# GNN and mixture-of-experts kernel: eight of nine additions of finished count tiles as adding transfers from GpSimd's queue

## The chip, the cores and the metric

The kernel runs on one core of one Trainium2 chip. The metric is device time in microseconds (us) of one execution. Differences of 0.5% or so are at the limit of what can be told from no change.

## What is computed

The reference takes x (1250 x 512), and 40000 edges src, dst. Cut to what matters:

```python
h = relu(layernorm(x) @ W1 + b1) @ W2 + b2          # 512 -> 256 -> 512
agg = segment_sum(h[dst], src)                      # row src[e] gets h[dst[e]]
x = x + h + agg
y = layernorm(x)
gate = softmax(y @ Wg + bg) - 0.25 * sigmoid(y @ Wt + bt)
w = max(gate, 0) / sum(max(gate, 0))                # 8 experts
x = x + sum_e w[e] * (y @ We[e] + be[e])
```

## The kernel before, in words

The edges are turned into a matrix of counts: entry (d, s) says how often node s takes from node d, plus one on the diagonal. The aggregation is then a dense product. The matrix has 1250 rows, in ten tiles of 125 (`TILES`), and each tile is made as five blocks (windows, `WPT`) of 25 rows, fifty in all (`NW`). For a block w

- VectorE (`compare`, L632) compares edge keys with positions and writes one-hot matrices into a ring of buffers,
- TensorE (`count`, L892 and L900) multiplies them and collects the counts in a PSUM bank, two banks in turn,
- ScalarE (`block_out`, L426) copies the bank to the buffer `counts[w % 5]`, once that buffer's last contents have been moved, and writes the positions of block w + 5 (L394),
- SP (L316) issues a copy of 125 KB from `counts[q]`, which lies as (position, 250), into 25 rows of the tile `a_t[i % 3]`. Three tiles are buffered; before the first block of tile i >= 3 SP waits until tile i - 3 has been aggregated (`g_done`) and summed.

TensorE takes up the aggregation of tile i (`aggregate`, L862: r_sb, the hidden layer, times the tile, added up in ps_g) ten blocks after the tile's first block, in pieces between the counting of blocks. Tiles 8 and 9 are aggregated after the last block, with no counting between.

The bias b2 enters with a factor, the number of terms a row has: the column sums of the whole count matrix. For this the ten tiles are added up in `a_sum` (125 x 1250, fp32; `column_sum`, L657), and ten small matmuls with a column of ones (L925) give the degrees. VectorE copies them (L678) and adds `b2 * degree` to x tile by tile (L684, ten instructions), before the output of the second layer is added (L692) and the second layer norm and the experts follow. In VectorE's program the additions of tiles 1 to 7 stand among the comparisons, that of tile 8 behind the last comparison, and that of tile 9 behind the low part of the first expert's weights (`low_weights`, L672). TensorE waits for the last addition after two of the six pieces of tile 9.

`a_t` and `a_sum` lie in the tensor `late`, and this is how the profile names them. The expert bias is broadcast to the same place afterwards (L321). GpSimd sets constants at the start and has nothing to do afterwards; it issues no transfer.

Of the kernel before, what the change touches and what calls it, by code (L numbers as in the profile page):

```python
# [16 lines left out]
ALU = mybir.AluOpType  # L17
# [13 lines left out]
def gnn_moe(nc, x, src, dst, W1, b1, W2, b2, Wg, bg, Wt, bt, We, be, out):  # L31
# [4 lines left out]
    TILES = 10  # L36
# [11 lines left out]
    WPT = 5  # L48
# [22 lines left out]
    with ExitStack() as ctx:  # L71
# [3 lines left out]
        def sem(name):  # L75
            return ctx.enter_context(nc.semaphore(name))
# [85 lines left out]
        a_t = [late[:, i * SW:(i + 1) * SW] for i in range(3)]  # L162
        a_sum = late[:, 3 * SW:4 * SW]
# [56 lines left out]
        step_base, step_ready, step_prep = sem("step_base"), sem("step_ready"), sem("step_prep")  # L220
        win_done, win_out = sem("win_done"), sem("win_out")
        win_moved = [sem(f"win_moved{q}") for q in range(WPT)]
        a_summed = sem("a_summed")
        g_done = sem("g_done")
        we_hi_done, we_lo_done = sem("we_hi_done"), sem("we_lo_done")
        wg_hi_done, wg_lo_done = sem("wg_hi_done"), sem("wg_lo_done")
# [43 lines left out]
        def moved(eng, tile):  # L270

            for q in range(WPT):
                eng.wait_ge(win_moved[q], 16 * (tile + 1))
# [11 lines left out]
        @block.sync  # L285
        def _(sp):
            sp.dma_start(dst_i[:, :, :], dst.rearrange("(j g e) -> g j e", j=GJ, e=EP)).then_inc(dst_in, 16)
            sp.dma_start(src_i[:, :, :], src.rearrange("(j g e) -> g j e", j=GJ, e=EP)).then_inc(src_in, 16)
            for j in range(TILES // 2):
                if j == 1:  # L290
                    sp.dma_start(w1_sb[:, :, :], W1.rearrange("(k p) c -> p k c", p=128)).then_inc(w1_in, 16)
                sp.dma_start(x_sb[0:112, 2 * j:2 * j + 2, :],
                             x[2 * j * R:(2 * j + 2) * R, :].rearrange("(t p) d -> p t d", p=R)[0:112, :, :]).then_inc(x_in[j], 16)
            sp.dma_start(b1_all[:, :], b1.partition_broadcast(R)).then_inc(b1_in, 16)

            def load_expert(e):
                sp.dma_start(stage[e % 2][:, :].rearrange("p (k f) -> p k f", k=KD),
                             We[e, :, :].rearrange("(k p) f -> p k f", p=128)).then_inc(we_in[e % 2], 16)

            sp.dma_start(w2_sb[:, :, :], W2.rearrange("(k p) c -> p k c", p=128)).then_inc(w2_in, 16)  # L300
            sp.dma_start(b2_sb[:, :], b2.partition_broadcast(R)).then_inc(b2_in, 16)
            sp.dma_start(wg_sb[:, :, 0:EXP], Wg.rearrange("(k p) c -> p k c", p=128)).then_inc(wg_in, 16)
            sp.dma_start(wg_sb[:, :, EXP:G1], Wt.rearrange("(k p) c -> p k c", p=128),
                         allow_slow_non_contiguous=True).then_inc(wg_in, 16)
            sp.dma_start(bg_sb[:, 0:EXP], bg.partition_broadcast(R)).then_inc(bg_in, 16)
            sp.dma_start(bg_sb[:, EXP:G1], bt.partition_broadcast(R)).then_inc(bg_in, 16)
            load_expert(0)
            load_expert(1)

            for w in range(NW):  # L310
                i, q = w // WPT, w % WPT
                sp.wait_ge(win_out, w + 1)
                if q == 0 and i >= 3:
                    sp.wait_ge(g_done, i - 2)
                    sp.wait_ge(a_summed, max(i - 3, 1))
                sp.dma_start(a_t[i % 3][q * WIN:(q + 1) * WIN, :].rearrange("p (h l) -> p h l", h=HI),  # L316
                             counts[q][0:WIN * HI, :]).then_inc(win_moved[q], 16)

            sp.wait_ge(g_done, TILES)
            sp.wait_ge(deg_done, 1)  # L320
            sp.dma_start(be_sb, be.rearrange("e f -> (e f)").partition_broadcast(R).rearrange("p (e f) -> p e f", e=EXP)).then_inc(be_in, 16)  # L321
            for e in range(2, EXP):
                sp.wait_ge(we_lo_done, e - 1)
                load_expert(e)

            for i in range(TILES):
                sp.wait_ge(acc_step, TILES * (EXP - 1) + i + 1 + RING)
                sp.dma_start(out[i * R:i * R + 112, :], x_sb[0:112, i, :]).then_inc(out_sent, 16)
            sp.wait_ge(out_sent, 32 * TILES)

        @block.gpsimd
        def _(pool):
# [26 lines left out]
            for n in range(len(STEPS) - 1, 0, -1):  # L359
# [4 lines left out]
                if len(STEPS) - len(FIXED) < n:  # L364
# [12 lines left out]
                                    base=-(HI - 1), pattern=[[1, SEG + HI - 1]], channel_multiplier=-HI).then_inc(self_ready, 1)  # L377
            nc.gpsimd.affine_select(out=self_lo[0:WIN, :], in_=self_lo[0:WIN, :], compare_op=ALU.not_equal, fill=1.0,
                                    base=-(LO - WIN), pattern=[[1, 2 * LO - WIN]], channel_multiplier=-1).then_inc(self_ready, 1)

        @block.scalar
        def _(act):
# [136 lines left out]
        def _(dve):  # L519
# [88 lines left out]
            def first_norm(n):  # L608

                if n == 0:  # L610
                    centre()
                if n < TILES // 2:
                    statistics(n)
                if n in RSTD_AT:
                    rstd(RSTD_AT[n])
# [33 lines left out]
                    step_done()  # L649
                dve.reg_mov(end_reg[w % 4], turn_reg)  # L650

            def column_sum(i):

                moved(dve, i)
                if i > 1:
                    dve.wait_ge(a_summed, i - 1)
                nc.vector.tensor_tensor(a_sum, a_t[0] if i == 1 else a_sum, a_t[i % 3], ALU.add).then_inc(a_summed, 1)  # L657

            for w in range(NW):
                compare(w)  # L660
                if w in NORM_AT:
                    first_norm(NORM_AT[w])
                if w >= 3 * WPT + 1 and (w - 1) % WPT == 0:
                    column_sum((w - 1) // WPT - 2)
            column_sum(TILES - 2)

            dve.wait_ge(wg_hi_done, 1)
            nc.vector.scalar_tensor_tensor(out=wg_2[:, :, G1:2 * G1], in0=wg_sb[:, :, :], scalar=WSCALE,
                                           in1=wg_2[:, :, 0:G1], op0=ALU.mult, op1=ALU.subtract).then_inc(wg_lo_done, 1)
            def low_weights(e, par):  # L670
                dve.wait_ge(we_hi_done, e + 1)
                nc.vector.scalar_tensor_tensor(out=we_lo[par][:, :], in0=stage[par][:, :], scalar=WSCALE, in1=we_hi[par][:, :],  # L672
                                               op0=ALU.mult, op1=ALU.subtract).then_inc(we_lo_done, 1)

            low_weights(0, 0)
            column_sum(TILES - 1)
            dve.wait_ge(deg_done, 1)
            nc.vector.tensor_copy(deg1[:, :], ps_a[0:R, 0:TILES]).then_inc(deg_ready, 1)  # L678
            dve.wait_ge(deg_ready, 1)
# [117 lines left out]
        def _(pe):  # L797
# [57 lines left out]
            def aggregate(i, first, last, closes=None):  # L855

                if first == 0:
                    moved(pe, i)
                    pe.wait_ge(r_ready, i + 1 if i > 0 else TILES)
                for n, (c, a, z) in enumerate(cuts[first:last]):  # L860
                    opens = i == 0 and (first + n == 0 or a // BANK != cuts[first + n - 1][1] // BANK)
                    g = nc.tensor.matmul(ps_g[:, a:z], r_sb[:, i, c * 128:(c + 1) * 128], a_t[i % 3][:, a - c * SW:z - c * SW],  # L862
                                         start=opens, stop=False, skip_group_check=True)
                    if n == 0 and closes is not None:
                        g.then_inc(win_done, 1)
                if last == len(cuts):
                    g.then_inc(g_done, 1)
# [52 lines left out]
                    aggregate((w - WPT - LAG) // WPT, piece, piece + 1 if piece < WPT - 1 else len(cuts), closes=w)  # L920
            aggregate(TILES - 2, WPT - LAG, len(cuts))
            aggregate(TILES - 1, 0, 2)
            pe.wait_ge(a_summed, TILES - 1)
            for i in range(TILES):
                dg = nc.tensor.matmul(ps_a[0:R, i:i + 1], a_sum[:, i * R:(i + 1) * R], ones[0:R, 0:1], start=True, stop=True)  # L925
            dg.then_inc(deg_done, 1)
# [108 lines left out]
```

## Time and profile before

| | |
|---|---|
| time, median of 3 runs | 393.59 us (392.02 to 393.86) |
| profiled execution | 392.6 us, its span 390.8 us |
| busy | TensorE 369.8, VectorE 286.8, ScalarE 105.3, GpSimd 6.1 us |
| counting and aggregation | from about 33 to 144 us |
| DMA | 23.87 MB in 16808 packets, mean 61 GB/s |

The span is what the profiler's records cover; the execution's own time is 1.8 us longer. Busy time is that of an engine's own instructions; waits and DMA issues don't count. The DMA share of a stretch is the mean busy share of the core's sixteen DMA engines.

### The profile page before, as it was taken

How to read it: one execution, taken by the hardware profiler on the slowest of the kernel's cores; microseconds unless marked ns; L12 is line 12 of the kernel's file. 1: busy time of each engine (PE TensorE's matmuls, PEld its weight loads, DVE VectorE, ACT ScalarE, POOL GpSimd, SP SyncE). 2: the span in 40 equal slices, each digit the busy share in tenths (PEclk: the TensorE clock that was granted, in tenths of full speed). 3: DMA queues.
4: the chain of work that ended last, by engine and by line, in shares of the span. 5: the costliest groups of instructions: out<-in, count | busy, mean ns of one | idle time of the engine just before them, and what ended most of it. 6: DMA issues, size and time to landing. Idle time of an engine off the chain costs nothing.

```text
span 390.8 us, 5935 instructions
## 1 busy us (share of the span) xinstructions
PE 369.8 (95%) x1892; PEld 240.8 (62%) x1892; DVE 286.8 (73%) x440; ACT 105.3 (27%) x189; POOL 6.1 (2%) x33
## 2 busy tenths in 40 slices
PE   0999999999999999979999999999999999999996
PEld 0777787656556563566566666666666666666663
DVE  3799987999988949872895756756767558566653
ACT  4734355556666204554001010010010100100000
POOL 6000000000000000000000000000000000000000
PEclk9999999999999999987999999999999999999999
DMA  8970011222222206300030020300301200000223
GB/s 175 243 239 17 15 39 37 78 67 80 74 73 83 83 14 160 132 28 2 1 107 2 10 99 0 108 0 0 107 0 23 84 0 0 0 0 0 68 91 105
DMA packets 16808, 23.87 MB, mean 61 GB/s; under 512 B 2796, under 2 KB 9683, under 8 KB 16660
## 3 DMA queue, kind: packets, MB, share of 16 engines
q1 hardware_dynamic: 16382, 23.05, 20.0%
q10 hardware_dynamic: 403, 0.53, 0.6%
q8 instruction: 12, 0.20, 0.2%
q14 instruction: 11, 0.09, 0.1%
HBM read 14.77 MB, written 2.56 MB: 44 GB/s over the span
## 4 chain that ended last, share of the span: by engine, by line
PE 80%; DVE 11%; issue 3%; DVEq 2%; DMA 1%; ACT 1%; ACTq 0%
PE ps_g L974 18%; PE ps_g L975 17%; PE ps_g L976 17%; PE ps_g L862 9%; PE ps_w L900 8%; DVE split L632 3%; PE ps_g L848 2%; PE ps_g L938 2%; DVE x_sb L684 2%; DVE stats L597 2%; DMA dst_i<-in_dst_dram 1%; PE ps_w L892 1%; PE ps_a L948 1%; DVEq L648 1%; PE ps_g L850 1%
## 5 line engine op out<-in xcount | busy, mean ns | idle before, releaser
L974 PE MATMUL ps_g<-we_hi,split 128*125 128x512 f16 x320 | 122.3, 382 | 0.4 <-DVE x_sb L758 0.4
L975 PE MATMUL ps_g<-we_lo,split 128*125 128x512 f16 x320 | 122.0, 381 | 0.0
L976 PE MATMUL ps_g<-we_hi,split 128*125 128x512 f16 x320 | 122.0, 381 | 0.0
L758 DVE SCALAR_TENSOR_TENSOR x_sb<-ps_g,weight_s,x_sb 125x512 f32<-125x512 f32 x80 | 59.9, 749 | 56.2 <-PE ps_g L976 56.1
L632 DVE TENSOR_TENSOR split<-places,keys 125x1536 f16<-125x1536 int16 (+2 forms) x125 | 91.3, 794 | 7.8 <-PE ps_w L900 4.2
L763 DVE SCALAR_TENSOR_TENSOR x_sb<-late,weight,x_sb 125x512 f32<-125x512 f32 x80 | 59.9, 750 | 9.5 <-DVE x_sb L758 5.5
L974 PEld LDWEIGHTS ps_g<-we_hi,split 128*125 128x125 f16 x320 | 44.1, 138 | 26.2 <-DVE x_sb L758 0.8
L976 PEld LDWEIGHTS ps_g<-we_hi,split 128*125 128x125 f16 x320 | 44.0, 137 | 25.8 <-issue 0.6
L975 PEld LDWEIGHTS ps_g<-we_lo,split 128*125 128x125 f16 x320 | 44.0, 138 | 25.4 <-issue 0.6
L900 PE MATMUL ps_w<-split 125*128 125x250 f16 x402 | 53.7, 270 | 3.4 <-DVE split L632 1.8
L900 PEld LDWEIGHTS ps_w<-split 125*128 125x128 f16 x402 | 36.8, 97 | 22.4 <-issue 9.7
L495 ACT ACTIVATE we_hi<-stage 128x2048 f16<-128x2048 f32 x6 | 11.5, 1912 | 139.8 <-PE ps_g L976 139.8
L862 PE MATMUL ps_g<-late,r_sb 125*128 125x512 f32 (+3 forms) x120 | 49.0, 515 | 0.0
L394 ACT ACTIVATE places<-iota_pos,win_base 125x512 int16<-125x512 int16 x50 | 35.7, 715 | 0.0
L426 ACT ACTIVATE counts<-ps_w 128x250 f32<-128x250 f32 x50 | 19.0, 380 | 32.7 <-PE ps_g L862 27.9
L862 PEld LDWEIGHTS ps_g<-late,r_sb 125*128 125x128 f32 x120 | 19.5, 191 | 7.7 <-issue 7.1
L848 PE MATMUL ps_g<-w_sb,x_t 128*125 128x256 f32 x80 | 19.6, 388 | 0.0
L672 DVE SCALAR_TENSOR_TENSOR we_lo<-stage,we_hi 128x2048 f16<-128x2048 f32 x8 | 18.3, 2284 | 0.0
L657 DVE TENSOR_TENSOR late<-late 125x1250 f32<-125x1250 f32 x9 | 13.1, 1456 | 4.4 <-DMA late<-counts 4.3
L848 PEld LDWEIGHTS ps_g<-w_sb,x_t 128*125 128x125 f32 x80 | 14.2, 187 | 1.8
L938 PE MATMUL ps_g<-w_sb,early 128*125 128x512 f32 x32 | 14.8, 595 | 0.1
L892 PE MATMUL ps_w<-self_lo,self_pos 128*128 128x250 f16 x50 | 13.6, 273 | 0.7 <-ACT counts L426 0.7
(129 smaller groups left out, 193.0 us busy)
## 6 DMA issues: line engine op xcount, KB each, us to landing
stage<-in_L_ffn_W_exp_dram SPq DMA_DIRECT2D x8, 1024.0 KB, 5.3
late<-counts SPq DMA_DIRECT2D x50, 122.1 KB
x_sb<-in_x_dram SPq DMA_DIRECT2D x5, 448.0 KB, 11.2
out_dram<-x_sb SPq DMA_DIRECT2D x10, 224.0 KB
late<-in_L_ffn_b_exp_dram SPq DMA_DIRECT2D x1, 2000.0 KB
w_sb<-in_L_gnn_W_dram SPq DMA_DIRECT2D x2, 512.0 KB, 11.6
x_sb<-in_x_dram ACTq DMA_DIRECT2D x1, 260.0 KB
out_dram<-x_sb ACTq DMA_DIRECT2D x10, 26.0 KB
```

The source lines that it names most:

```text
L394: nc.scalar.activation(places[w % WPT][:, :, 0:SEG], iota_pos[:, :, :], ACT.Identity, bias=win_base[:, w:w + 1], scale=1.0).then_inc(pos_r ...
L426: nc.scalar.activation(counts[q][:, :], ps_w[w % 2][:, 0:LO], ACT.Copy).then_inc(win_out, 1)
L632: nc.vector.tensor_tensor(hot[hot_at(w, p)][:, 0:n, :].rearrange("p c (k x j) -> p (c k) x j", k=SEGS, j=2), places[w % WPT][:, 0:n, :].re ...
L758: nc.vector.scalar_tensor_tensor(out=x_sb[:, i, :], in0=ps_exp[(TILES * par + i) % RING], scalar=weight_s[:, ds(e, 1), i], in1=x_sb[:, i, ...
L763: nc.vector.scalar_tensor_tensor(out=x_sb[:, i, :], in0=be_sb[:, ds(e, 1), :], scalar=weight[:, i, ds(e, 1)], in1=x_sb[:, i, :], op0=ALU.m ...
L848: nc.tensor.matmul(r_bank[i % 2], x_t[i % XTS][:, k, :], w1_sb[:, k, :], start=(k == 0), stop=False)
L862: g = nc.tensor.matmul(ps_g[:, a:z], r_sb[:, i, c * 128:(c + 1) * 128], a_t[i % 3][:, a - c * SW:z - c * SW], start=opens, stop=False, ski ...
L900: mm = nc.tensor.matmul(bank[:, 0:LO], hot[hot_at(w, p)][:, c, 0:SEG], hot[hot_at(w, p)][:, c, SEG:SEG + LO], start=False, stop=False, ski ...
L938: y = nc.tensor.matmul(ps_y[i % YS], g_sb[:, c, tokens[i]], w2_sb[:, c, :], start=(c == 0), stop=(c == KC - 1))
L974: nc.tensor.matmul(bank, xhi[:, k, tokens[i]], hi_w, start=(k == 0), stop=False)
L975: nc.tensor.matmul(bank, xhi[:, k, tokens[i]], lo_w, start=False, stop=False)
L976: mm = nc.tensor.matmul(bank, xlo[:, k, tokens[i]], hi_w, start=False, stop=(k == KD - 1))
```

## The change

A semaphore `a_added` is new. GpSimd, after its constants, issues nine transfers of whole tiles (125 x 1250 fp32): tile 0 is copied to `a_sum`, tiles 1 to 8 are added to it by the transfer (`accum_op=ALU.add`). Each waits until its tile's five blocks have landed and until the transfer before it is complete. VectorE keeps the addition of tile 9, at its old place, and waits there for all nine. SP waits for the transfers instead of VectorE's sums before it fills a buffer again. TensorE waits for the one count that VectorE now gives.

```diff
--- before.py
+++ after.py
@@ -220,7 +220,7 @@
         step_base, step_ready, step_prep = sem("step_base"), sem("step_ready"), sem("step_prep")
         win_done, win_out = sem("win_done"), sem("win_out")
         win_moved = [sem(f"win_moved{q}") for q in range(WPT)]
-        a_summed = sem("a_summed")
+        a_added, a_summed = sem("a_added"), sem("a_summed")
         g_done = sem("g_done")
         we_hi_done, we_lo_done = sem("we_hi_done"), sem("we_lo_done")
         wg_hi_done, wg_lo_done = sem("wg_hi_done"), sem("wg_lo_done")
@@ -312,7 +312,7 @@
                 sp.wait_ge(win_out, w + 1)
                 if q == 0 and i >= 3:
                     sp.wait_ge(g_done, i - 2)
-                    sp.wait_ge(a_summed, max(i - 3, 1))
+                    sp.wait_ge(a_added, 16 * (i - 2))
                 sp.dma_start(a_t[i % 3][q * WIN:(q + 1) * WIN, :].rearrange("p (h l) -> p h l", h=HI),
                              counts[q][0:WIN * HI, :]).then_inc(win_moved[q], 16)
 
@@ -377,6 +377,13 @@
                                     base=-(HI - 1), pattern=[[1, SEG + HI - 1]], channel_multiplier=-HI).then_inc(self_ready, 1)
             nc.gpsimd.affine_select(out=self_lo[0:WIN, :], in_=self_lo[0:WIN, :], compare_op=ALU.not_equal, fill=1.0,
                                     base=-(LO - WIN), pattern=[[1, 2 * LO - WIN]], channel_multiplier=-1).then_inc(self_ready, 1)
+
+            for i in range(TILES - 1):
+                moved(pool, i)
+                if i > 0:
+                    pool.wait_ge(a_added, 16 * i)
+                nc.gpsimd.dma_start(a_sum[:, :], a_t[i % 3][:, :],
+                                    accum_op=ALU.bypass if i == 0 else ALU.add).then_inc(a_added, 16)
 
         @block.scalar
         def _(act):
@@ -649,20 +656,10 @@
                     step_done()
                 dve.reg_mov(end_reg[w % 4], turn_reg)
 
-            def column_sum(i):
-
-                moved(dve, i)
-                if i > 1:
-                    dve.wait_ge(a_summed, i - 1)
-                nc.vector.tensor_tensor(a_sum, a_t[0] if i == 1 else a_sum, a_t[i % 3], ALU.add).then_inc(a_summed, 1)
-
             for w in range(NW):
                 compare(w)
                 if w in NORM_AT:
                     first_norm(NORM_AT[w])
-                if w >= 3 * WPT + 1 and (w - 1) % WPT == 0:
-                    column_sum((w - 1) // WPT - 2)
-            column_sum(TILES - 2)
 
             dve.wait_ge(wg_hi_done, 1)
             nc.vector.scalar_tensor_tensor(out=wg_2[:, :, G1:2 * G1], in0=wg_sb[:, :, :], scalar=WSCALE,
@@ -673,7 +670,9 @@
                                                op0=ALU.mult, op1=ALU.subtract).then_inc(we_lo_done, 1)
 
             low_weights(0, 0)
-            column_sum(TILES - 1)
+            moved(dve, TILES - 1)
+            dve.wait_ge(a_added, 16 * (TILES - 1))
+            nc.vector.tensor_tensor(a_sum, a_sum, a_t[(TILES - 1) % 3], ALU.add).then_inc(a_summed, 1)
             dve.wait_ge(deg_done, 1)
             nc.vector.tensor_copy(deg1[:, :], ps_a[0:R, 0:TILES]).then_inc(deg_ready, 1)
             dve.wait_ge(deg_ready, 1)
@@ -920,7 +919,7 @@
                     aggregate((w - WPT - LAG) // WPT, piece, piece + 1 if piece < WPT - 1 else len(cuts), closes=w)
             aggregate(TILES - 2, WPT - LAG, len(cuts))
             aggregate(TILES - 1, 0, 2)
-            pe.wait_ge(a_summed, TILES - 1)
+            pe.wait_ge(a_summed, 1)
             for i in range(TILES):
                 dg = nc.tensor.matmul(ps_a[0:R, i:i + 1], a_sum[:, i * R:(i + 1) * R], ones[0:R, 0:1], start=True, stop=True)
             dg.then_inc(deg_done, 1)
```

## Rows read from the trace of the kernel before

**Rows 1.** The page, parts 1, 2 and 4: engines, slices, chain.
```profile
PE 369.8 (95%) x1892; PEld 240.8 (62%) x1892; DVE 286.8 (73%) x440; ACT 105.3 (27%) x189; POOL 6.1 (2%) x33
...
POOL 6000000000000000000000000000000000000000
...
PE 80%; DVE 11%; issue 3%; DVEq 2%; DMA 1%; ACT 1%; ACTq 0%
```

**Rows 2.** Chain of waits, 103 to 144 us (start, us, what).
```profile
103.19 0.54 PE ps_w L900 x5
...
107.19 0.19 issue
107.38 0.38 ACT counts L426
...
127.44 0.54 PE ps_w L900 x5
...
131.49 0.43 issue
...
133.21 0.26 issue
...
134.17 7.60 PE ps_g L862 x20
141.77 2.09 PE ps_a L925 x20
```

**Rows 3.** The chain, 60 to 84 us.
```profile
78.75 0.93 DVE late L657
...
81.95 0.60 PE ps_w L900 x4
```

**Rows 4.** Timeline, 130 to 156 us (start, length, what, idle before).
```profile
129.55 3.11 DVE L632 TENSOR_TENSOR split<-places,keys 125x768 f16<-125x768 int16 x5
...
134.06 2.28 DVE L672 SCALAR_TENSOR_TENSOR we_lo<-stage,we_hi 128x2048 f16<-128x2048 f32 x1
...
139.79 1.46 DVE L657 TENSOR_TENSOR late<-late 125x1250 f32<-125x1250 f32 x1 [3.45 <-DMA late<-counts]
...
144.09 6.71 DVE L684 SCALAR_TENSOR_TENSOR x_sb<-b_sb,deg,x_sb 125x512 f32<-125x512 f32 x10
...
146.47 0.29 SPq L321 DMA_DIRECT2D late<-in_L_ffn_b_exp_dram  x1
...
146.81 0.39 SPq L297 DMA_DIRECT2D stage<-in_L_ffn_W_exp_dram  x1
```

**Rows 5.** One line's instructions, L657: duration min/median/max in ns.
```profile
L657 DVE TENSOR_TENSOR late<-late x9: 1451/1454/1461, 78.7 to 139.8; 125x1250 f32<-125x1250 f32 x9
```

**Rows 6.** Timeline, 81 to 83.5 us.
```profile
81.09 0.42 PEld L900 LDWEIGHTS ps_w<-split 125*128 125x128 f16 x4 [0.33 <-DVE split L632]
...
81.95 0.33 PEld L900 LDWEIGHTS ps_w<-split 125*128 125x128 f16 x4 [0.43 <-DVE split L632]
81.95 0.60 PE L900 MATMUL ps_w<-split 125*128 125x250 f16 x4 [0.16 <-DVE split L632]
```

**Rows 7.** Timeline of SP's queue, three of the fifty count copies.
```profile
68.46 0.74 SPq L316 DMA_DIRECT2D late<-counts  x1
...
127.07 0.74 SPq L316 DMA_DIRECT2D late<-counts  x1
...
135.54 0.74 SPq L316 DMA_DIRECT2D late<-counts  x1
```

**Rows 8.** Stretches: length, busy (instructions) by engine, granted clock, DMA share, GB/s.
```profile
core 0: us, PE busy (x) PEld busy (x) DVE busy (x) ACT busy (x) POOL busy (x), PEclk, DMA share, GB/s
100.00:130.00 30.00, 28.77 (x157) 17.53 (x156) 27.43 (x42) 19.25 (x38) 0.00 (x0) 1.00 0.27 80
160.00:165.00 5.00, 5.00 (x33) 2.96 (x32) 4.21 (x13) 2.94 (x6) 0.00 (x0) 1.00 0.31 134
160.00:180.00 20.00, 17.85 (x107) 11.75 (x106) 12.97 (x37) 10.23 (x20) 0.00 (x0) 0.83 0.13 53
```

## The prediction

> **What bounds the kernel now.** I read the page first: TensorE is busy for 95% of the span, VectorE for 73%, GpSimd for 2%, and the chain of work that ended last is 80% TensorE and 11% VectorE [rows 1]. The change touches only the stretch from about 58 to 150 us, so I asked for the chain of waits there. Between 103 and 134 us it is TensorE's counting and aggregation matmuls, broken by "issue" and ScalarE pieces of 0.1 to 0.4 us, and no VectorE piece [rows 2]. VectorE stands in it only before 82 us, where the first addition has 0.93 us [rows 3]. Behind the last block the order turns around: ten accumulations end at 141.77, the degree matmuls (L925) run to 143.86, VectorE copies the degree, and its ten L684 instructions fill 144.09 to 150.80 (6.71 us) [rows 2, 4]. That is the tail: whoever delays the full sum delays everything behind it, one for one. So two questions decide: does anything in 58 to 134 us wait for an addition now, and is the sum ready as early as before?
>
> The profiled execution took 392.6 us, 1.8 more than its span of 390.8, and 1.0 less than the median of 393.59. I add the change to 392.6 and carry the difference over to the median.
>
> **What is removed.** Eight of nine VectorE additions at 1.454 us, 11.6 us in all [rows 5]. In rows 2 none of them is on the chain. At 82 us there is one real stall: TensorE idles 0.16 us for VectorE's comparisons at 81.95, and weight loads before it are held 0.33 and 0.43 us [rows 6]; the first addition, 3 us earlier, pushed those comparisons back. I book a gain of 0.2 us, and at most 0.93. Later VectorE is ahead: its comparisons of the last block ended at 129.55 + 3.11 = 132.66, and TensorE took them up at 133.47 [rows 4]. Behind the last comparison the eighth addition lies before the weights' low part L672, which ends at 136.34, and VectorE then idles 3.45 us for the last transfer [rows 4]: nothing to gain. What is late next, in each of these places, is TensorE itself.
>
> **What is added.** One copy and eight adding transfers of 125 rows of 5000 bytes, 625 KB each, on GpSimd's queue. GpSimd has nothing behind them: it does 6.1 us of work in all [rows 1]. But three others wait for them:
> - each addition waits for the one before (same destination), so they form a row of nine;
> - SP waits for addition i-3 before it issues the first count copy of tile i. Behind that instruction stand all later count copies, for which ScalarE (reuse of the count buffer) and TensorE (accumulation) wait;
> - VectorE waits for the ninth before its own last addition, and TensorE's degree matmuls wait for that; behind them are the last four accumulations of tile 9.
>
> The trace has no adding DMA, so I bound its length A. Fixed part: the last count copy is issued at 135.54 and VectorE can go on at 139.79, 4.25 us later [rows 4, 7]. One such copy is 125 KB on five engines (below), 25 KB each, which at 18.5 GB/s is 1.35 us; so 2.9 us are fixed. Moving part: an addition has to read two tiles and write one, 1.25 MB of reads. Rates: from 160 to 165 us what is left of the loads issued at 146.5 and 146.8 [rows 4] is the broadcast of the expert bias, with a DMA share of 0.31, that is 5.0 of 16 engines, and 134 GB/s: 26.8 GB/s per busy engine. From 100 to 130 us the count copies have a share of 0.27 (4.3 engines) at 80 GB/s: 18.5 GB/s per busy engine [rows 8]. On sixteen engines the moving part is 1.25 MB / 16 = 78 KB per engine, 2.9 us at the first rate and 4.2 at the second; if the second operand were free, 1.5 us. On five it is 250 KB, 9.3 to 13.5 us. So A is between 2.9 + 1.5 = 4.4 and 2.9 + 13.5 = 16.4. I take sixteen engines, the split that favours the change, and A = 6.5; five is a rival. In time alone this is hidden: tile 1 is complete at 68.46 + 4.25 = 72.7 us, the last sum begins at 139.8, eight additions in a row fit as long as A is under (139.8 - 72.7) / 8 = 8.4 us; tile 8 is complete at 127.07 + 4.25 = 131.3, and with 6.5 its addition ends at 137.8.
>
> One rule speaks to the choice. The bias rows are 125 to a transfer, and it ran on 5.0 engines [rows 8]. The Trainium skill, "DMA: Bandwidth & Descriptors", section "Why a DMA increments its semaphore by 16 and not by 1", says the number of engines is the largest divisor up to 16 of the outer dimension; by that rule, the trace agrees (125 gives 5). The same section says that GpSimd's queue gives some direct copies all sixteen with the rows rounded up per engine; no row here shows it. The first would make the addition the rival of five engines (about 424 us), the second leaves the forecast.
>
> **The engines are the scarce part.** The count copies are on five engines, which are therefore 86% busy (4.3 of 5) in the stretch [rows 8]. The time per tile is three tiles from 103.19 to 127.44, 8.1 us each [rows 2]. On each of the five engines a tile's copies take 125 KB, 6.8 us at 18.5 GB/s; part of that is waiting inside a packet, since at 26.8 GB/s it would be 4.7. An addition on sixteen engines lays 2.9 to 4.2 us on the same five. The sum is 7.6 at best, below 8.1: nothing is late; 11.0 at worst, 2.9 too much. I take the middles, 5.8 + 3.55 = 9.35: 1.25 us too much per tile. Seven tiles (2 to 8) pass while an addition runs, so the last tile lands 8.75 us late. First the copies' time to landing eats this up, then ScalarE's wait for a free count buffer holds TensorE back, but both ways the last landing is late by all of it, because there is no room in the tail: accumulations of tile 9 begin at 141.77 - 1.72 (four pieces of 0.43) = 140.05, and its last copy lands at 139.79: 0.3 us [rows 2, 4]. The final sum ends at 141.25 against 141.77, 0.5 us.
>
> Sum: + 8.75 - 0.3 (room) - 0.2 (VectorE's stall) = + 8.2, rounded to 8. 392.6 + 8 = 400.6 for an execution like the profiled one, 393.59 + 8 = 401.6 against the median. Own range of this case: + 3 (1.25 replaced by 0.5) to + 20 (2.9 per tile), so 396.6 to 413.6. TensorE would idle for some microseconds in such a stall; the mean granted clock, 1.00 in the rows before, is 0.83 from 160 to 180 us [rows 8], where TensorE is busy for 17.85 of 20 us. A second such stretch, at the same lost share (0.17 of 20 us), would add 3.4 us; it is in the range, not in the sum.
>
> A second rule bears on the read of both tiles. The Trainium skill, "Collectives: The Full Stack", section "The bandwidth ceiling: the fold count and why AG ≠ RS ≠ AR", says that a DMA engine's addition costs a second source read and not the arithmetic. No row here shows it. By it the 2.9 stands; if the second read were free the load would be 5.8 + 1.5 = 7.3, under 8.1, and the next rival would be the forecast.
>
> **Rivals.**
> - *Hidden.* The additions fit into the gaps of the five engines (7.6 us or less per tile). For it: a share of 0.27 with 18.5 GB/s means that the packets wait for each other, and another queue could use that time. Against: 86% busy. In the tail the ninth addition shares the engines with the last three copies, 2.9 us at most, of which I let 1 us reach the landing: + 1.0 - 0.2 = + 0.8, 394.4 us.
> - *Row of nine too long.* The adding transfer runs on five engines as the bias load does. A = 2.9 + 9.3 = 12.2, over the 8.4 from which it decides; the ninth ends at 72.7 + 8 x 12.2 = 170.3, 30.5 late. SP's wait holds the copies back meanwhile, but the row is the longer. 393.6 + 30.5 = 424 us; at the slower rate (A = 16.4) 64 late, 457.6.
> - *Faster.* VectorE was behind TensorE's small stalls after all. The chain's pieces that are not matmul between 107.15 and 133.47 are ten, of 0.02 to 0.43 us (the longer ones stand in [rows 2]), 1.9 us together, and with the 0.2 it is 2.1: 391.5 us. It decides if no comparison is ready when TensorE asks. Against: a comparison is 0.8 us ahead in the last block, and the pieces stand behind the shortest accumulations, where TensorE waits for ScalarE to free a bank. This is the other side.
> - *Not what it says:* GpSimd could reach its first transfer late, so that nothing overlaps. Its own work is 6.1 us, all of it in the first of 40 slices [rows 1], so I give this nothing.
>
> **How the numbers follow.** Forecast 0.40, of which 0.04 comes out within 0.5%; hidden 0.28, 0.25 of it within 0.5% and 0.03 above; five engines 0.24; faster 0.08, of which 0.06 by over 0.5% and 0.02 under. An effect of 0.5%, 2.0 us, is about what a measurement of this kernel can tell from none. Hence faster 0.06; within 0.31; slower 0.63. The range goes from 392.8, which leaves out about 0.09 below (the faster case and the edge of the hidden one), to 426, which leaves out the part of the five-engine case with the slower rate, about 0.11.
>
> **What would show it.** The DMA queue of GpSimd in the queue table, nine issues, and the DMA share of 100 to 130 us: 0.45 or more if sixteen engines work, under 0.35 if five. Copies' landings: the idle of VectorE before its last sum, 3.45 us before, longer by the loss, put down to the landing of a count copy (forecast) or to the adding transfer (row too long). Time per tile in the chain: 8.1 if hidden, above 9 in the last tiles if the engines are full. VectorE's busy time should fall by 11.6 us and the 0.16 us at 82 should go. The forecast is wrong if the share stays far below 0.45 while the tiles keep their 8.1 us, and the start of the degree matmuls, 141.77, is within 1 us of that.

## The result, and the profile after

The changed kernel takes 425.92 us (median of four, 422.17 to 427.94) against 392.80 before (four executions); the ratio is 1.084, 95% interval 1.0785 to 1.0896: 33 us slower. The profiled execution took 427.94 us, its span 426.1 us against 390.8. Ratios leave out an execution that was slow against others of its kernel: of e5's ten one (992.65 us), and e4, with one of its two slow, has no ratio.

The page of the changed kernel, parts 1 to 4 (busy time; the span in 40 slices; DMA queues; the chain):

```profile
PE 381.7 (90%) x1892; PEld 245.2 (58%) x1892; DVE 277.5 (65%) x432; ACT 105.2 (25%) x189; POOL 13.5 (3%) x42
...
DMA  8860132675676665063000202020020300000133
...
q1 hardware_dynamic: 16382, 23.05, 18.4%
q0 software_dynamic: 1296, 5.63, 11.4%
...
PE 67%; DMA 21%; DVE 6%; issue 3%; DVEq 1%; ACT 1%; ACTq 0%; POOLq 0%
PE ps_g L973 16%; PE ps_g L975 16%; PE ps_g L974 16%; DMA late<-counts 14%; DMA late<-late 5%; PE ps_w L899 4%; PE ps_g L937 3%; PE ps_g L861 3%; DVE split L639 2%; PE ps_g L847 2%; DVE stats L604 1%; DMA dst_i<-in_dst_dram 1%; PE ps_w L937 1%; ACT counts L433 1%; PE ps_a L924 1%
```

DMA is now 21% of the chain (1% in [rows 1]), and most of it, 14%, is put down not to the new transfers but to the old count copies (`late<-counts`). VectorE's busy time is 9.3 us less, not 11.6: the additions are gone, but its other instructions, the comparisons among them, take somewhat longer. The chain in the stretch (start, length in us), which answers to [rows 2]:

```profile
73.50 12.52 DMA late<-counts
...
91.63 8.77 DMA late<-counts
...
102.15 11.04 DMA late<-counts
...
120.30 9.41 DMA late<-counts
...
130.13 8.18 DMA late<-counts
...
138.74 11.55 DMA late<-counts
...
150.39 13.44 DMA late<-late
...
164.39 7.77 DMA late<-late
...
172.28 1.47 DVE late L675
...
173.80 3.11 PE ps_a L924 x20
176.91 5.14 PE ps_g L861 x8
```

The count copies on the chain take 8 to 12.5 us. From issue to landing, all copies issued from the first addition on (72.67) take 4.3 to 14.4 us; before, the longest took 4.75. They queue behind each other, up to five at a time. The degree matmuls, at 141.77 before [rows 2], start at 173.80: 32.0 us of the span's 35.3. The other 3.3 lie behind them. There the degree matmuls take 3.11 us instead of 2.09, and the granted clock is down while TensorE waits (stretches as in [rows 8]: length, busy time by engine, clock, DMA share, GB/s):

```profile
100.00:130.00 30.00, 23.84 (x122) 13.97 (x122) 17.57 (x28) 15.80 (x31) 2.51 (x3) 0.94 0.73 118
160.00:176.00 16.00, 6.73 (x24) 3.44 (x22) 1.46 (x1) 0.00 (x0) 0.83 (x1) 0.76 0.42 66
```

The DMA share of 100 to 130 us has risen from 0.27 to 0.73. GpSimd's queue gives the time per tile (start, length of the issue, and the wait before it):

```profile
100.95 0.84 POOL L385 DMA_DIRECT2D late<-late  x1 [11.30 <-DMA late<-counts]
112.33 0.83 POOL L385 DMA_DIRECT2D late<-late  x1 [10.54 <-DMA late<-counts]
...
136.75 0.83 POOL L385 DMA_DIRECT2D late<-late  x1 [12.42 <-DMA late<-counts]
150.39 0.84 POOL L385 DMA_DIRECT2D late<-late  x1 [12.81 <-DMA late<-counts]
164.39 0.83 POOL L385 DMA_DIRECT2D late<-late  x1 [13.16 <-DMA late<-counts]
```

From one issue to the next it is 16.1 and 12.2 us for the first two intervals (from the issue at 72.67), then 11.9 each for three, and 13.6 and 14.0 for the last two, against 8.1 before. An adding transfer takes 11.5 us from issue to landing (the page's median; 10.6 to 13.4, and 7.8 for the last).

The profile says that GpSimd waited for count copies. The landings in the trace (the semaphore's events) say otherwise from tile 4 on: the tile had landed, and the transfer was issued 0.56 us after the one before it had landed.

| tile | its copies landed | transfer before landed | issued |
|---|---|---|---|
| 2 | 88.16 | 85.14 | 88.80 |
| 4 | 108.39 | 111.77 | 112.33 |
| 6 | 132.30 | 136.19 | 136.75 |
| 8 | 154.22 | 163.83 | 164.39 |

So the last 60 us before the final sum are the row of transfers, one after the other, and the count copies are late beside it. At the end (TensorE, then VectorE):

```profile
168.17 3.74 PE L861 MATMUL ps_g<-late,r_sb 125*128 125x512 f32 x4 [7.38 <-DMA late<-counts]
173.80 3.11 PE L924 MATMUL ps_a<-ones,late 125*125 125x1 f32 x20 [1.89 <-DVE late L675]
172.28 1.46 DVE L675 TENSOR_TENSOR late<-late 125x1250 f32<-125x1250 f32 x1 [25.11 <-DMA late<-late]
```

The last count copy lands at 167.93, 28.4 us later than before (139.57). Less the 0.3 us of room, plus 2.0 for the four accumulations at the lower clock (3.74 instead of 1.72 us) and TensorE's wait of 1.89 us for the sum, that makes the 32.0 us.

### The profile page after: what moved, and what is told of

Same layout as the page of the kernel before. It is cut to its first block, busy times and chain, and to the rows that moved or that the text cites. A ratio compares the mean times of both kernels' runs of the same rounds, so it can differ in the third digit from the quotient of the medians.

```text
span 426.1 us, 5933 instructions
## 1 busy us (share of the span) xinstructions
PE 381.7 (90%) x1892; PEld 245.2 (58%) x1892; DVE 277.5 (65%) x432; ACT 105.2 (25%) x189; POOL 13.5 (3%) x42
## 3 DMA queue, kind: packets, MB, share of 16 engines
q1 hardware_dynamic: 16382, 23.05, 18.4%
## 4 chain that ended last, share of the span: by engine, by line
PE 67%; DMA 21%; DVE 6%; issue 3%; DVEq 1%; ACT 1%; ACTq 0%; POOLq 0%
PE ps_g L973 16%; PE ps_g L975 16%; PE ps_g L974 16%; DMA late<-counts 14%; DMA late<-late 5%; PE ps_w L899 4%; PE ps_g L937 3%; PE ps_g L861 3%; DVE split L639 2%; PE ps_g L847 2%; DVE stats L604 1%; DMA dst_i<-in_dst_dram 1%; PE ps_w L937 1%; ACT counts L433 1%; PE ps_a L924 1%
## 5 line engine op out<-in xcount | busy, mean ns | idle before, releaser
L639 DVE TENSOR_TENSOR split<-places,keys 125x1536 f16<-125x1536 int16 (+2 forms) x125 | 92.4, 795 | 29.4 <-PE ps_w L899 11.4
L899 PE MATMUL ps_w<-split 125*128 125x250 f16 x402 | 55.0, 277 | 11.5 <-issue 9.3
L861 PE MATMUL ps_g<-late,r_sb 125*128 125x512 f32 (+3 forms) x120 | 54.7, 566 | 8.4 <-DMA late<-counts 8.4
L502 ACT ACTIVATE we_hi<-stage 128x2048 f16<-128x2048 f32 x6 | 11.5, 1911 | 139.4 <-PE ps_g L975 139.4
L861 PEld LDWEIGHTS ps_g<-late,r_sb 125*128 125x128 f32 x120 | 21.6, 210 | 18.3 <-issue 16.5
L891 PE MATMUL ps_w<-self_lo,self_pos 128*128 128x250 f16 x50 | 14.1, 281 | 6.6 <-ACT counts L433 6.6
L675 DVE TENSOR_TENSOR late<-late 125x1250 f32<-125x1250 f32 x1 | 1.5, 1461 | 25.1 <-DMA late<-late 25.1
## 6 DMA issues: line engine op xcount, KB each, us to landing
late<-late POOLq DMA_DIRECT2D x9, 610.4 KB, 11.5
```

The source lines that it names most:

```text
L639: nc.vector.tensor_tensor(hot[hot_at(w, p)][:, 0:n, :].rearrange("p c (k x j) -> p (c k) x j", k=SEGS, j=2), places[w % WPT][:, 0:n, :].re ...
L899: mm = nc.tensor.matmul(bank[:, 0:LO], hot[hot_at(w, p)][:, c, 0:SEG], hot[hot_at(w, p)][:, c, SEG:SEG + LO], start=False, stop=False, ski ...
```

## The experiments

Theory A: the transfers fill the DMA engines that the count copies need, and the copies land late whether anyone waits for a sum or not. Theory B: the engines have room; the loss is in the waits, nine transfers in a row, SP's wait and VectorE's. The edits are shown shortened: setup, and semaphore counts that follow from the edit, are left out.

**e1, the load without the waits.**

```diff
+ junk_in, junk_sum = sb("junk_in", [R, SW]), sb("junk_sum", [R, SW])
  (kernel before; on GpSimd:)
+ for i in range(TILES - 1):
+     moved(pool, i)
+     if i > 0: pool.wait_ge(a_added, 16 * i)
+     nc.gpsimd.dma_start(junk_sum, junk_in, accum_op=bypass if i == 0 else add).then_inc(a_added, 16)
```

> The kernel before, with VectorE's nine additions and all its waits, plus nine extra transfers of the same size from GpSimd's queue, triggered by the same landings, but between two spare tiles of their own; nothing waits for them. Theory A, full engines: in the changed kernel a row of 5000 bytes that is added holds a DMA engine for 0.65 to 0.75 us (its packets), eight rows are 6.0 us on each of sixteen engines, and with the 5.8 to 6.8 us of a tile's count copies on five of them that is 12 to 13 us per 8.1 us tile; so the load alone must cost most of the 33 us: 410 to 426. Theory B, the waits: each addition takes about 11 us, over the 8.4 that fit in a row of nine, and SP and VectorE wait for them; without waits the time is that of before, 391 to 395.

423.28 us, ratio 1.078 (1.0705 to 1.0862). The load alone, between tiles that nobody reads, costs nearly what the change costs (31.2 us of 33, with overlapping intervals); waits are not needed for the loss, and B is out as the main cause. The chain holds the same long count copies, and no transfer of GpSimd's:

```profile
73.56 12.62 DMA late<-counts
...
93.27 9.11 DMA late<-counts
102.80 9.81 DMA late<-counts
...
126.25 11.75 DMA late<-counts
```

**e2, the waits without the load.**

```diff
- nc.gpsimd.dma_start(a_sum[:, :], a_t[i % 3][:, :], ...)
+ part = SW if i == 0 else 25
+ nc.gpsimd.dma_start(a_sum[:, 0:part], a_t[i % 3][:, 0:part], ...)
```

> The changed kernel with all its waits; the copy of tile 0 stays whole, the eight additions take 25 of 1250 columns (the rest of the sum is left out, so the degrees are wrong). Theory A: with 100 bytes per row the engines are free, 391 to 395. Theory B says the same if the length of an addition is what counts. Theory C, that the waits, the issue from GpSimd's queue and the turn from one transfer to the next cost by themselves (some 4 us each, on SP's path): 397 or more.

392.53 us, ratio 1.000 (0.997 to 1.004). Waiting on GpSimd's queue costs nothing by itself; theory C is out.

**e3 and e4, the dose.** The same edit with `accum_op=ALU.bypass` for all nine, and with `part = SW // 2`.

> The changed kernel with all nine transfers as plain copies (nothing is added, the degrees are wrong): same rows, same waits. The one copy in the changed kernel held an engine 0.35 us per row. Theory A: 8 rows x 0.35 to 0.45 = 2.8 to 3.6 us, with 5.8 to 6.8 of the count copies 9 to 10 per tile against 8.1: 1 to 2 us x 7 tiles, 400 to 407. Theory B: the copy took 5.5 us from issue to landing, under 8.4: 392 to 395.

> The changed kernel, the copy of tile 0 whole, the eight additions over 625 of 1250 columns (half of the sum is left out). Theory A: 8 rows x 0.37 = 3 us per engine, like the plain copies: 399 to 407. Theory B: an addition takes about 6 to 7 us, under the 8.4 that fit: 392 to 395. If the cost is per row and not per byte, 415 or more.

Copies: 406.85 us, ratio 1.037 (1.031 to 1.042). Half the columns: 397.0 and 403.9 us in two runs, too far apart for an interval, both above before. The copies are where A put them (400 to 407) and B did not; of the halves one run is in A's 399 to 407, the other 2 us under it and 2 above B's. A copy and half an addition take nearly the same time on an engine (e6), and in the traces the last count copy is late by nearly the same: 8.3 and 7.0 us.

**e6, the price by itself.** The kernel before, with seven transfers between spare tiles late in the expert phase.

```diff
+ pool.wait_ge(exp_done, 55)
+ copy 125x1250; add 125x1250; copy; add; add 125x625; add 125x25; add 125x1250 with max_dma_last_dim=1000
+ (each after the one before)
```

> The kernel before; in the late expert phase, where no other transfer is under way, GpSimd issues seven transfers between two spare tiles, one after the other: copy, addition, copy, addition of 125 x 1250, addition of 125 x 625, of 125 x 25, and an addition of 125 x 1250 cut into 1000-byte pieces. If an addition is slow by itself: 8 rows x 0.7 us + 3 = 8 to 9 us against 5.5 for the copy, 5 to 6 for the half. If it was slow only because of the count copies beside it: 6 us. The cut one: about 8.5 on sixteen engines, 20 on five. Time of the kernel as before, 390 to 394.

GpSimd's queue (start, issue, wait before):

```profile
322.76 0.75 POOL L391 DMA_DIRECT2D junk_sum<-junk_in  x1 [314.14 <-PE ps_g L989]
328.03 0.90 POOL L391 DMA_DIRECT2D junk_sum<-junk_in  x1 [4.52 <-DMA junk_sum<-junk_in]
336.00 0.55 POOL L391 DMA_DIRECT2D junk_sum<-junk_in  x1 [7.07 <-DMA junk_sum<-junk_in]
...
348.95 0.84 POOL L391 DMA_DIRECT2D junk_sum<-junk_in  x1 [7.07 <-DMA junk_sum<-junk_in]
353.72 0.83 POOL L391 DMA_DIRECT2D junk_sum<-junk_in  x1 [3.93 <-DMA junk_sum<-junk_in]
356.06 3.10 POOL L391 DMA_DIRECT2D junk_sum<-junk_in  x1 [1.50 <-DMA junk_sum<-junk_in]
```

The kernel's time is that of before (one execution, 392.64 us). Start to start: the copy 5.3 us, the addition 8.0, the half 4.8, the 25 columns 2.3. The engines' rate within a transfer (clock, DMA share, GB/s at the end of each row; first an addition, then a copy, then half an addition):

```profile
330.00:335.00 5.00, 5.00 (x25) 3.17 (x24) 3.01 (x4) 0.00 (x0) 0.00 (x0) 1.00 0.91 108
337.50:339.50 2.00, 2.00 (x11) 1.28 (x10) 1.50 (x2) 0.00 (x0) 0.00 (x0) 1.00 1.02 255
...
351.00:353.00 2.00, 2.00 (x11) 1.23 (x9) 1.85 (x3) 0.00 (x0) 0.00 (x0) 1.00 0.89 115
```

With nothing beside it an addition fills 0.91 of sixteen engines at 108 GB/s, 625 KB in 5.8 us; a copy runs at 255 GB/s, 2.45 us; half an addition at 115, 2.7 us. (A share of 1.02 shows that packets can overlap in this count; it is rough.) So the slow addition of the changed kernel is not only slowed by its neighbours: 8.0 of its 11.5 us are its own. The cut one took 19.1 us to land, with transfers of the kernel's own beside it from 365 us on; the share does not say on how many engines.

**e7, smaller rows.**

```diff
+ for h in range(HI):
+     nc.gpsimd.dma_start(a_sum[:, h * LO:(h + 1) * LO], a_t[i % 3][:, h * LO:(h + 1) * LO], ...)
```

> The changed kernel, each tile's transfer issued as five transfers of 125 x 250 (1000 bytes per row) that are under way together. Same bytes, same rule of who waits. If the loss is the bytes' time on the engines (5.6 us of additions + 5.8 of copies per 8.1 us tile): 415 to 428 again. If it is that a count packet of 46 ns stands behind one addition row of 0.6 us each time, the smaller rows let the copies through: 395 to 408.

432.37 us, ratio 1.101 (1.092 to 1.111), above both ranges. The smaller rows do let count copies through while an addition runs. The trace has a record for each packet. Those of 1000 bytes on the copies' queue from 75 to 81 us, during the first addition:

| kernel | count packets in 6 us |
|---|---|
| before | 401 |
| changed (rows of 5000 bytes) | 35 |
| e7 (rows of 1000 bytes) | 190 |

In the changed kernel 105 rows of the addition pass in the same time; a third of them, 33, would be on five of sixteen engines (an estimate), so one count packet goes through for about each row. But no time is gained in e7: from tile 3 on each tile's transfers are issued when those of the tile before have landed, and they take 11 to 15 us (the last ones 7.3). The bytes' time stays, and five issues per tile keep GpSimd busy for 11.23 of the 30 us from 100 on. Rows of 1000 bytes on sixteen engines, without the waits, were not tried.

**e8, fewer engines at a time.** e1 with `max_dma_last_dim=1000`.

> As the load-only kernel (nothing waits for the extra transfers), but each cut into 1000-byte pieces, which I expect to put it on five engines instead of sixteen, not always the five of the count copies. If the loss comes from sharing DMA engines, only those transfers cost that meet the copies' five engines, so a third or less of the 31 us: 394 to 404, with most copies landing in 3.3 to 4.5 us. If it comes from the memory or the fabric in common, 415 or more.

418.76 us, ratio 1.067 (1.059 to 1.074); I expected 394 to 404, and missed. By its time alone the run speaks for the rival, a memory or a path in common (415 or more). What is seen in the trace speaks against it: between 66 and 170 us count copies hold the chain three times, twice while the fourth transfer is under way (issued at 115.09) and once during the fifth (140.26), and never during the second and third. First the chain, then GpSimd's queue:

```profile
117.73 9.36 DMA late<-counts
127.52 10.52 DMA late<-counts
145.47 12.49 DMA late<-counts
```

```profile
75.21 3.03 POOL L389 DMA_DIRECT2D junk_sum<-junk_in  x1 [14.99 <-DMA late<-counts]
93.83 3.02 POOL L389 DMA_DIRECT2D junk_sum<-junk_in  x1 [15.60 <-DMA late<-counts]
115.09 3.02 POOL L389 DMA_DIRECT2D junk_sum<-junk_in  x1 [18.24 <-DMA late<-counts]
140.26 3.03 POOL L389 DMA_DIRECT2D junk_sum<-junk_in  x1 [22.16 <-DMA late<-counts]
```

Two stretches, during the second transfer and during the fourth (clock, DMA share, GB/s of all queues at the end):

```profile
79.00:92.00 13.00, 12.13 (x73) 7.53 (x70) 13.00 (x18) 6.42 (x14) 0.00 (x0) 1.00 0.63 110
119.00:136.00 17.00, 13.52 (x63) 6.86 (x62) 9.59 (x15) 6.27 (x13) 0.00 (x0) 0.91 0.41 71
```

In the first, 62 count packets go through per microsecond (67 before, in the same stretch); in the second 35 (80 before), though less moves in all, 71 against 110 GB/s. A memory in common that was full would hold the copies where most moves. That some transfers hurt and others don't fits engines shared or not; where a transfer does meet the copies, it holds them for some 20 us, which my estimate lacked. The records of the trace don't name the engine, so this stays a reading. The last count copy lands 18.4 us late; the rest of the 26.8 us lies behind it, and what it is wasn't looked into.

**e9, SP's wait relaxed.** `late` one tile larger, `a_t[i % 4]`, SP waits from tile 4 on for addition i - 4.

> The changed kernel with four buffered count tiles instead of three, so that SP waits for the addition of tile i-4 before it fills a buffer. Theory A, full engines: SP's wait is a symptom, the engines stay full, 418 to 427. Theory B, what is left of it: SP's wait (10.1 us in the trace of the changed kernel) and TensorE behind it; then 10 us less, 412 to 418.

424.10 us, ratio 1.080 (1.074 to 1.087): the interval overlaps that of the changed kernel. SP's wait is worth nothing that can be told in the whole time. In the trace it does show: the last count copy lands at 162.58, not 167.93, but VectorE then still waits for the ninth transfer, to 167.21.

**e5, VectorE relieved, nothing put in its place.**

```diff
-                if w >= 3 * WPT + 1 and (w - 1) % WPT == 0:
-                    column_sum((w - 1) // WPT - 2)
-            column_sum(TILES - 2)
  (SP's wait for the sums goes too)
```

> The kernel before without the first eight additions and without any transfer in their place: VectorE adds tiles 8 and 9 once, at the end (the rest of the sum is left out). This is the most that relieving VectorE can bring. My step: 0.2 us, at most 0.93, so a ratio of 0.998 to 1.001. Rival, the small stalls of TensorE between 103 and 134 us were VectorE's: 2 us less, ratio 0.995.

Ratio 1.001 (0.998 to 1.003). Eight additions on VectorE cost nothing, so there was nothing to win by moving them anywhere.

**e10, GpSimd's own adder.**

```diff
- nc.gpsimd.dma_start(a_sum, a_t[i % 3], accum_op=...)
+ nc.gpsimd.tensor_tensor(a_sum, a_t[0] if i == 1 else a_sum, a_t[i % 3], ALU.add)
```

> The kernel before with tiles 1 to 8 added by GpSimd's own tensor_tensor instead of VectorE's, tile 9 by VectorE; no transfer. VectorE's relief is worth nothing (the run without any addition), so if GpSimd needs under 8.1 us per tile and doesn't hold up VectorE, the ratio is 0.998 to 1.003. Rival: GpSimd and VectorE block each other at the comparisons, which read two tiles too; then up to 8 times one addition's length on VectorE where it has no lead (72 to 100 us), 2 to 8 us more, 1.005 to 1.02.

403.81 us, ratio 1.027 (1.022 to 1.031), worse than either expectation. The chain runs over one instruction, the first of these:

```profile
72.44 19.43 POOL L385 TENSOR_TENSOR late<-late 125x1250 f32<-125x1250 f32 x1 [64.90 <-DMA late<-counts]
92.03 2.40 POOL L385 TENSOR_TENSOR late<-late 125x1250 f32<-125x1250 f32 x1 [0.17 <-POOL late L385]
100.20 2.84 POOL L385 TENSOR_TENSOR late<-late 125x1250 f32<-125x1250 f32 x1 [5.77 <-DMA late<-counts]
```

The first addition takes 19.43 us, the others 2.40 to 4.11. It falls into the stretch in which VectorE compares without pause, and SP waits 14.1 us for it. The Trainium skill, "SBUF — State Buffer", section "Who interferes with whom", says that a VectorE instruction with two inputs from the buffer contends with a GpSimd instruction that reads it; the trace agrees, 19.43 against 2.40 us. No run has this addition without the comparisons beside it.

**e11 and e12, a shorter tail.** The chain behind the degrees has ten L684 instructions where only seven fit before the first output tile. Three were moved among the layer norm's steps (e11), or given to GpSimd (e12).

```diff
- for i in range(TILES): (b2 times degree, tile i)
+ for i in range(7): ...
+ e11, in turn_over(i): if 2 <= i <= 4: add_b2(i + 5)
+ e12, on GpSimd: tensor_scalar, then tensor_tensor, for tiles 7 to 9
```

> The kernel before; VectorE's ten L684 instructions (b2 times degree, 6.7 us on the chain from the degrees to 150.8 us) become seven at the old place, and three that stand between the first steps of the second layer norm. The first output tile is there at 148.9 us, when seven are done (148.8). If VectorE has room in the layer norm stretch: 1 to 2 us less, ratio 0.995 to 0.998. If VectorE bounds that stretch: no change, 0.999 to 1.001.

> The same three tiles' b2 times degree on GpSimd instead, in two instructions each, while VectorE does the other seven. GpSimd has from 144 to 160 us for them. If it doesn't hold up VectorE: 2 us less, ratio 0.994 to 0.997. If they block each other on their way to the buffers: 0.998 to 1.005.

e11: ratio 0.998 (0.996 to 1.000), at the edge of what can be told; e12: 0.999 (0.997 to 1.001). In e12 VectorE's seven instructions took longer than the ten before (6.71 us, [rows 4]), beside GpSimd's:

```profile
143.12 7.62 DVE L692 SCALAR_TENSOR_TENSOR x_sb<-b_sb,deg,x_sb 125x512 f32<-125x512 f32 x7
```

e11 is the only version that may be faster than before, and it owes nothing to the change.

## Why the prediction was wrong

The direction and the main mechanism, full engines, were right; the size was not: 8 us forecast, 33 measured, outside the likeliest case's own range (up to 20). Two steps failed: the length of an addition, and the reading that the row of nine is hidden.

- *VectorE's relief, 0.2 us.* Right: e5 shows none that can be measured.
- *Sixteen engines or five.* Right. An addition of 125 rows alone fills 0.91 of sixteen (e6). The Trainium skill, "DMA: Bandwidth & Descriptors", section "Why a DMA increments its semaphore by 16 and not by 1", makes this exception for some direct copies on GpSimd's queue; by that rule, the trace agrees, for an addition too.
- *The engines are the scarce part.* Right as a mechanism: e1 has the loss without the waits, e2 the waits without the loss.
- *An addition lays 2.9 to 4.2 us on each engine; middle 3.55.* The first term that failed. It measured 5.8 us (e6). I had doubled the bytes and taken rates of 18.5 to 26.8 GB/s per engine from other transfers. A copy from buffer to buffer with these rows already runs at 255 GB/s, 16 per engine, and an addition takes 2.4 times as long. Of the Trainium skill's rule that an addition costs a second read ("Collectives: The Full Stack", section "The bandwidth ceiling: the fold count and why AG ≠ RS ≠ AR") the trace shows 2.4 for its 2; the rate to which I applied it was the fault.
- *The count copies take 5.8 us, the middle between 4.7 and 6.8.* Not refuted. When copies are queued and nothing else runs, as here in e3, they move at 108 GB/s, which is 5.8 us for a tile's 625 KB:

```profile
92.00:95.00 3.00, 3.00 (x17) 1.79 (x16) 2.49 (x4) 1.85 (x4) 0.52 (x1) 1.00 0.34 108
```

  With the measured addition, 5.8 + 5.8 = 11.6, 3.5 over the 8.1, times seven tiles is 24.5 us. In e1, where nobody waits, the last count copy lands at 163.34, 23.8 us late, and in e9 23.0 us late. The sum is rough all the same: for plain copies (2.45) and half additions (2.7) it gives 1 and 3 us, and 8.3 and 7.0 were measured; with 6.8 for the copies it would give 8 and 10 there, but 31.5 for the additions.
- *The row of nine, hidden in time.* The second step that failed. I compared 6.5 us with the threshold of 8.4. An addition alone takes 8.0 us from issue to issue, just under it, but beside the count copies 11.9: the full engines lengthen the row as well. From tile 4 on it sets when the transfers go out, SP stands 10.1 us for two of them, and VectorE and TensorE wait for the ninth. In the profiled executions the last count copy is 28.4 us late with SP's wait and 23.8 or 23.0 without it (e1, e9), and TensorE waits 1.9 us more for the sum. In the whole time the waits can't be told from nothing: e9 and e1 have 1.080 and 1.078 beside 1.084, with overlapping intervals, 2 to 3 us by the medians. The two paths are nearly as long as each other, and whoever shortens one meets the other.
- *The rival of five engines.* It had A = 12.2 and the ninth addition's end at 170.3; measured 11.9 and 172.2. Its row of nine is there, its reason (five engines) is not, and e1 loses nearly as much without the row's waits. That 425.92 still lies inside the full range, to 426, is owed to this rival, whose length comes out right for a wrong reason: that is luck.
- *The granted clock.* I left a second slow stretch, 3.4 us, out of the sum and in the range. It came, 3.3 us, behind the stall: TensorE stood still for most of 160 to 176 us.
- *Signs named.* A DMA share of 0.45 or more for sixteen engines (0.73) and tiles above 9 us (11.9) came. VectorE's idle time before its last sum grew from 3.45 to 25.11 us, but the profile puts it down to the adding transfer, which I had named as the sign of the row too long, not of the forecast. VectorE's busy time fell by 9.3 us, not 11.6. The stall at 82 us now lies under the first long copy and can't be judged.

Open stays how the engines divide themselves between two queues. One count packet for about each added row fits the counts at 75 to 81 us, but the records don't name the engine; and why plain copies and half additions delay the count copies by more than the sum says isn't shown.

## What to carry to other kernels

Work that is moved to a transfer is paid in engine time: take the busy share of those DMA engines that are in use (five here, at 86% by their packets, or 80 of the 108 GB/s that queued copies reach), not the mean over sixteen (0.27), and add the new transfer's time on each. A row of transfers that wait for each other is compared with the room it has at the length it takes beside the others (11.9 us), not alone (8.0). An adding transfer costs over twice a copy of the same bytes. When the profile puts a wait on one of several semaphores, compare it with the landings. And before relieving an engine, take its work away altogether once: if that brings nothing, as in e5, no place for it will.

## What was not expected of the hardware

- An addition by transfer, 125 rows of 5000 bytes in the buffer: 8.0 us from issue to the next, 108 GB/s; the plain copy 5.3 us, 255 GB/s; 100 bytes a row 2.3 us.
- While rows of 5000 bytes are added, 35 count packets go through in 6 us, and 190 when the rows have 1000 bytes; without an addition 401.
- A GpSimd tensor_tensor of 125 x 1250 took 19.43 us beside VectorE's unbroken comparisons, and 2.40 to 4.11 us otherwise; VectorE's seven L692 took 7.62 us beside GpSimd's, where the ten before took 6.71.
